# Cross attention: 32x32 squares for the results, and one turn of the maxima for two groups

## The reference, cut to what matters

```python
    def _L0_xattn_ref(values, keys, query, mask, Wv, Wk, Wq, Wo, bo):
        v = (values @ Wv.T).reshape(N, Lv, HEADS, HEAD_DIM)   # Lv = 375, 16 heads of 16
        k = (keys @ Wk.T).reshape(N, Lk, HEADS, HEAD_DIM)
        q = (query @ Wq.T).reshape(N, Lq, HEADS, HEAD_DIM)
        energy = jnp.einsum('nqhd,nkhd->nhqk', q, k)
        energy = jnp.where(mask == 0, jnp.float32(-1e+20), energy)
        attention = jax.nn.softmax(energy / jnp.sqrt(jnp.float32(E)), axis=3)
        out = jnp.einsum('nhql,nlhd->nqhd', attention, v).reshape(N, Lq, E)
        return out @ Wo.T + bo
```

## Time and profile before

| what | value |
|---|---|
| median of 3 runs | 1869.5 us (1869.06 to 1873.52) |
| profiled execution, its own time | 1868.54 us |
| its span, first to last instruction | 1867.2 us |
| mean granted clock of TensorE | 0.984 |
| PE busy | 1796.4 us (96%) |
| DVE busy | 1188.1 us (64%) |
| ACT busy | 692.4 us (37%) |
| POOL busy | 655.4 us (35%) |

### The profile page before, as it was taken

How to read it: one execution, slowest core, us unless ns; L and a number is a source line. 1 busy time by engine, 2 the same in 40 slices (tenths; PEclk the granted TensorE clock), 3 DMA queues, 4 the chain that set the end, 5 groups by cost and what they waited for, 6 DMA issues and landing times.

```text
span 1867.2 us, 39141 instructions
## 1 busy us (share of the span) xinstructions
PE 1796.4 (96%) x14764; PEld 1301.2 (70%) x14764; DVE 1188.1 (64%) x3209; ACT 692.4 (37%) x1812; POOL 655.4 (35%) x694
## 2 busy tenths in 40 slices
PE   6789999999989999999999999999999999999999
PEld 5457777776766666665445666666659979799698
DVE  4778888887657777777766676777764234243332
ACT  2234444443435555553001456565532122122221
POOL 2524444243226676664000366666624000000000
PEclk7989999999989999999999999999999999999999
DMA  6222212221031111110000010010040000000000
GB/s 202 48 42 42 45 30 42 41 37 26 13 118 52 34 45 37 33 44 12 1 1 1 11 33 23 22 32 22 12 181 1 8 3 1 11 1 1 11 1 10
DMA packets 106953, 61.94 MB, mean 33 GB/s; under 512 B 79944, under 2 KB 102800, under 8 KB 106000
## 3 DMA queue, kind: packets, MB, share of 16 engines
q1 hardware_dynamic: 106624, 59.39, 12.0%
q10 hardware_dynamic: 144, 0.06, 0.0%
HBM read 53.91 MB, written 5.51 MB: 32 GB/s over the span
## 4 chain that ended last, share of the span: by engine, by line
PE 79%; DVE 6%; issue 5%; POOL 5%; ACT 2%; DMA 2%; SPq 1%; DVEq 0%; ACTq 0%; POOLq 0%
PE ps L2515 18%; PE ps L1529 6%; PE ps L588 6%; PE ps L1551 5%; PE ps L2387 5%; PE ps L2047 5%; PE ps L1600 4%; PE ps L1568 4%; PE ps L2593 3%; PE ps L704 2%; POOL w L560 2%; PE ps L1585 2%; PE ps L1666 2%; PE ps L1538 2%; PE ps L1611 1%
## 5 line engine op out<-in xcount | busy, mean ns | idle before, releaser
L1960 POOL TENSOR_TENSOR h_w<-h_w 125x336 int32<-125x336 int32 x384 | 335.3, 902 | 205.1 <-ACT h_w L1759 205.1
L1845 DVE CUSTOM_DVE_ANT_0 h_w<-ps,h_w 112x375 f32<-112x375 f32 x512 | 262.7, 542 | 0.3 <-issue 0.3
L922 DVE SCALAR_TENSOR_TENSOR big_b<-ps,taps,big_b 128x444 f32<-128x444 f32 (+2 forms) x288 | 193.9, 674 | 55.6 <-ACT big_b L804 43.8
L1759 ACT ACTIVATE h_w<-ps 125x336 f32<-125x336 f32 x512 | 196.5, 464 | 21.9 <-PE ps L1551 21.7
L276 POOL TENSOR_TENSOR rstd<-var_eps,minus_half 112x4 f32<-112x4 f32 x12 | 12.2, 1016 | 406.5 <-DVE var_eps L263 406.5
L1551 PEld LDWEIGHTS ps<-h_w 32*125 32x125 f32 x3072 | 97.8, 184 | 68.6 <-issue 67.8
L1551 PE MATMUL ps<-h_w 32*125 32x112 f32 x3072 | 118.7, 283 | 12.4 <-DVE h_w L1845 8.3
L1529 PE MATMUL ps<-h_w 32*112 32x375 f32 x1024 | 121.0, 522 | 0.9 <-DVE h_w L1845 0.7
L588 PE MATMUL ps<-h_w,kq_w 128*128 128x448 f32 x256 | 112.3, 564 | 5.5 <-DVE h_w L942 5.5
L2047 PE MATMUL ps<-expert_w,big_a 128*112 128x512 f32 x256 | 113.6, 595 | 0.0
L1854 DVE TENSOR_TENSOR h_w<-h_w,ps 128x112 f32<-128x112 f32 x128 | 34.8, 272 | 121.6 <-PE ps L1538 121.6
(11 more groups left out here) (362 smaller groups left out, 3682.6 us busy)
## 6 DMA issues: line engine op xcount, KB each, us to landing
h_w<-in_h SPq DMA_DIRECT2D x2, 4096.0 KB, 17.6
kq_w<-in_ctxT SPq DMA_DIRECT2D x16, 375.0 KB, 3.7
h_w<-in_ctxT SPq DMA_DIRECT2D x16, 375.0 KB, 3.8
big_a<-decays SPq DMA_DIRECT2D x16, 196.0 KB, 3.1
w<-decays SPq DMA_DIRECT2D x16, 196.0 KB, 3.1
h_w<-in_mask SPq DMA_DIRECT2D x16, 164.1 KB
h_w<-in_maskT SPq DMA_DIRECT2D x16, 164.1 KB
kq_w<-in_kq_w SPq DMA_DIRECT2D x8, 256.0 KB, 3.1
```

Of the source, the lines that this page charges most:

```text
L922: dve.scalar_tensor_tensor(p3(dst)[:, :, i:], p3(ps[:, bank, 0:GT])[:, :, 0:T - i], k.taps[:, h, n, TAPS - 1 - i:TAPS - i], p3(dst)[:, :, ...
L1759: act.activation(k.PTx[(4 * Q + r) % RING][0:CK], ps[0:CK, turned_bank(Q, r), 0:NC * T], ACT.Exp).then_inc(s["exp"], 1)
L1845: dve.tensor_tensor_reduce(k.masked[r % 2], ps[0:T, score_bank(Q, r), 0:S2], k.mask_add[n % 2], -1.0, 3.0e38, ALU.add, ALU.min, k.neg_max[ ...
L1960: pool.tensor_tensor(P.bitcast(I32), P.bitcast(I32), k.mask_W[n % 2], ALU.mult).then_inc(s["weights"], 1)
```

## The change

- **32x32 squares.** DVE's transpose turns each 32x32 square. `apply` now writes each group to 128 columns of bank 6 (112 used; DVE sets the rest to 1.0 once, in the first step). `tokens` (DVE, step 3, for the sequence before) transposes bank 6, 128x512, to `o_tok` with tokens in the 32-row squares. `normalize` works on that on 128 partitions. `channels` (DVE, step 0, for the sequence two back) transposes 128x256 back to `onT` in layer 0; in layer 1 to `on_raw`, and ACT adds the bias to make `onT`, in `middle` of step 0. `output_turn`, `output_back` and ACT's copy of bank 6 are gone. The output weight keeps its own row order.
- **One turn for two groups.** `maxima` runs in steps 0 and 2 only and turns the columns of two groups, which stand in 16-column halves of the same tile. `less_maximum` becomes a `scalar_tensor_tensor` with a column of `k_keep` that keeps one half's rows, twice in a row.
- **One step later.** In step s, `maxima` and `turned` are of group s - 2, `apply` of s - 3. ACT, DVE and POOL shift alike, and each loop's tail with its first gates or experts does too. The first score of a group is ahead of the turn on PE, and the first maximum ahead of `less_maximum` on DVE. The banks of the turned scores move by two, and the waits with them.
- **Queries and values.** The last piece of the values is no longer part of `queries`: `values_2` stands at the end of step 2 and waits for the query copy. ACT copies it at the start of step 3.
- `mask_weights` moves from step 2 to step 3 on DVE.

```diff
+    turned = k.big_b[:, 0:2, :].rearrange("p a b -> p (a b)")
+    k.o_tok, k.on = turned[:, 0:XH * SQUARE], turned[:, XH * SQUARE:XH * SQUARE + XH * XD]
+    k.onT, k.on_raw = k.big_b[:, 2, 0:KD * 4 * SQUARE], k.big_b[:, 3, 0:KD * 4 * SQUARE]
@@ -1303,7 +1304,12 @@
...
-    return (8 * Q + 12 + r) % POOL_BANKS
+    return r if Q == QUADS * B - 1 else (8 * Q + 2 + r) % POOL_BANKS
@@ -1502,7 +1508,7 @@
...
-    def scores(seq, q):
...
-        for r in range(4):
+        for r in heads:
             if Q == 0 and r == 1:
                 pe.wait_ge(s["k_sb"], 4)
             if r < 2 and Q:
                 pe.wait_ge(s["max"], 4 * Q - 1 + r)
-            elif r >= 2 and Q >= 2:
-                pe.wait_ge(s["exp"], 4 * Q - 9 + r)
+            elif r >= 2 and Q >= 3:
+                pe.wait_ge(s["exp"], 4 * Q - 13 + r)
...
-        pe.wait_ge(s["max"], 4 * Q + 4)
+        pe.wait_ge(s["max"], 4 * Q + 8)
         if Q:
             pe.wait_ge(s["exp"], 4 * Q - 1)
-        pe.transpose(ps[:, turned_bank(Q, 0), NC * T:(NC + 1) * T], k.neg_max[:, q % 2, :], k.ident[0:T, 0:T]).then_inc(s["max_T"], 1)
+        pe.transpose(ps[:, turned_bank(Q, 0), NC * T:(NC + 1) * T], k.neg_max[:, Q // 2 % 2, :], k.ident[0:T, 0:T]).then_inc(s["max_T"], 1)
...
-        pe.wait_ge(s["qx"], Q + 1)
+        pe.wait_ge(s["qx"], Q + 1 if Q % 2 else Q + 2)
         if Q:
             pe.wait_ge(s["exp"], 4 * Q)
-        if Q < last:
-            pe.wait_ge(s["max"], 4 * Q + 6)
+        if Q < last - 1:
+            pe.wait_ge(s["max"], 4 * Q + 10)
@@ -1561,11 +1567,13 @@
...
             pe.wait_ge(s["V"], 2 * (n + 1))
             if n:
-                pe.wait_ge(s["oa"], n)
+                pe.wait_ge(s["o_tok"], n)
+            else:
+                pe.wait_ge(s["setup_dve"], 6)
...
-                ins = pe.matmul(ps[32 * r:32 * r + 32, 6, q * T:(q + 1) * T], k.Vx[n % 2][0:rows, c, 4 * q + r, :],
+                ins = pe.matmul(ps[32 * r:32 * r + 32, 6, q * 128:q * 128 + T], k.Vx[n % 2][0:rows, c, 4 * q + r, :],
@@ -1605,12 +1609,18 @@
...
-        pe.wait_ge(s["ctx_sum"], n + 1)
         for m in range(KD):
             for c in range(KD):
-                pe.matmul(ps[:, 7, m * T:(m + 1) * T], w["q"][:, c, m * 128:(m + 1) * 128], k.xT[:, c, 0:T],
-                          start=(c == 0), stop=(c == KD - 1))
-        values(n, 2, KD * T).then_inc(s["q_proj"], 1)
+                ins = pe.matmul(ps[:, 7, m * T:(m + 1) * T], w["q"][:, c, m * 128:(m + 1) * 128], k.xT[:, c, 0:T],
+                                start=(c == 0), stop=(c == KD - 1))
+        ins.then_inc(s["q_proj"], 1)
+
+    def values_2(seq):
+
+        n = base + seq
+        pe.wait_ge(s["ctx_sum"], n + 1)
+        pe.wait_ge(s["qz"], n + 1)
+        values(n, 2, KD * T).then_inc(s["v2_proj"], 1)
@@ -1630,40 +1640,17 @@
...
-    def output_turn(seq):
-        n = base + seq
-        pe.wait_ge(s["oa"], n + 1)
-        if is_sequence(seq + 2):
-            pe.wait_ge(s["qz"], n + 3)
-            pe.wait_ge(s["V"], 2 * n + 5)
-        elif is_sequence(seq + 1):
-            pe.wait_ge(s["V"], 2 * n + 4)
-            if l == 0:
-                pe.wait_ge(s["lnT_act"], LN_MOE + 1)
...
-        for i in range(QUADS):
-            ins = pe.transpose(ps[0:T, 7, i * 128:(i + 1) * 128], k.oa[:, i * T:(i + 1) * T], k.ident[:, :])
-        ins.then_inc(s["c_oT"], 1)
-
-    def output_back(seq):
-        n = base + seq
-        pe.wait_ge(s["on"], n + 1)
-        if seq == B - 2:
-            pe.wait_ge(s["lnT_dve"], (LN_MOE + 1, LN_FFN + KD)[l])
-        for c in range(KD):
-            ins = pe.transpose(ps[:, 7, c * T:(c + 1) * T], k.on[:, c * 128:(c + 1) * 128], k.ident[0:T, 0:T])
-        ins.then_inc(s["onT_ps"], 1)
-
     def output(seq):
         n = base + seq
         pe.wait_ge(s["onT"], n + 1)
         if is_sequence(seq + 2):
             pe.wait_ge(s["k_sb"], 4 * n + 12)
+        elif is_sequence(seq + 1):
+            pe.wait_ge(s["lnT_dve"], (LN_MOE + 1, LN_FFN + KD)[l])
+        else:
+            pe.wait_ge(s["c_x"], n)
         for c in range(KD):
-            ins = pe.matmul(ps[0:T, 7, 0:D], k.onT[:, c * T:(c + 1) * T], w["o"][:, c, :],
+            ins = pe.matmul(ps[0:T, 7, 0:D], k.onT[:, c * 128:c * 128 + T], w["o"][:, c, :],
@@ -1695,28 +1685,26 @@
...
-        elif q == 2 and is_sequence(seq - 1):
-            output_turn(seq - 1)
-        elif q == 3 and is_sequence(seq - 1):
-            if is_sequence(seq + 1):
-                pe.wait_ge(s["k_sb"], 4 * n + 6)
-            output_back(seq - 1)
+        elif q == 2 and is_sequence(seq + 1):
+            values_2(seq + 1)
 
     for step in range((B + 1) * QUADS + 1):
         seq, q = quad_at(step)
-        before, b_q = quad_at(step - 1)
-        ago, a_q = quad_at(step - 2)
+        before, b_q = quad_at(step - 2)
+        ago, a_q = quad_at(step - 3)
         if step == 1:
             values_first()
         if is_sequence(seq):
-            scores(seq, q)
-        if is_sequence(before):
+            scores(seq, q, (0,))
+        if is_sequence(before) and b_q % 2 == 0:
             maxima(before, b_q)
+        if is_sequence(seq):
+            scores(seq, q, (1, 2, 3))
         if step:
             early(seq, q)
         if is_sequence(before):
             turned(before, b_q)
-        if (seq, q) == (B, 1):
+        if (seq, q) == (B, 2):
             pe.wait_ge(s["exp"], (l + 1) * B * XH)
...
-        if (seq, q) == (B, 2):
+        if (seq, q) == (B, 3):
             if l == 0:
                 gating_pe(pe, k, s, 0, 12)
                 expert_pe(pe, k, s, 0, 2)
+                expert_pe(pe, k, s, 0, 3)
             else:
                 ffn_pe_gate(pe, k, s, 0, 2)
-        elif (seq, q) == (B, 3):
-            if l == 0:
-                expert_pe(pe, k, s, 0, 3)
-            else:
                 ffn_pe_gate(pe, k, s, 0, 3)
@@ -1762,6 +1747,11 @@
+    def values_2(seq):
+
+        n = base + seq
+        act.wait_ge(s["v2_proj"], n + 1 - (l + 1))
         if n >= 2:
             act.wait_ge(s["PV"], 4 * (n - 1))
         act.activation(k.Vx[n % 2][0:CK + 1, 2, :, 0:XD], heads_of(ps[0:CK + 1, 7, KD * T:KD * T + D]), ACT.Copy).then_inc(s["V"], 1)
@@ -1777,36 +1767,22 @@
-        elif q == 3:
-            if is_sequence(seq - 1):
-                act.wait_ge(s["onT_ps"], n)
-                if n >= 2:
-                    act.wait_ge(s["o_proj"], n - 1)
-                if l == 0:
-                    ins = act.activation(k.onT, ps[:, 7, 0:KD * T], ACT.Copy)
-                else:
-                    for c in range(KD):
-                        ins = act.activation(k.onT[:, c * T:(c + 1) * T], ps[:, 7, c * T:(c + 1) * T], ACT.Identity,
-                                             bias=k.xb_col[:, 2, c:c + 1])
-                ins.then_inc(s["onT"], 1)
+        elif l and q == 0 and is_sequence(seq - 2):
+            act.wait_ge(s["on_raw"], seq - 1)
+            act.wait_ge(s["o_proj"], n - 2)
+            for c in range(KD):
+                ins = act.activation(k.onT[:, c * 128:c * 128 + T], k.on_raw[:, c * 128:c * 128 + T], ACT.Identity, bias=k.xb_col[:, 2, c:c + 1])
+            ins.then_inc(s["onT"], 1)
...
-        before, b_q = quad_at(step - 1)
+        before, b_q = quad_at(step - 2)
...
-            if is_sequence(seq - 1):
-                act.wait_ge(s["PV"], 4 * n)
-                if n >= 2:
-                    act.wait_ge(s["c_oT"], n - 1)
-                act.activation(k.oa, ps[:, 6, 0:GT], ACT.Copy).then_inc(s["oa"], 1)
...
+            values_2(seq + 1)
             cross_keys_act(act, k, s, l, seq + 1, 0, 7)
@@ -1836,22 +1816,23 @@
         Q = 4 * n + q
         if q == 0 and r == 0:
             dve.wait_ge(s["mask"], n + 1)
-        if r == 0 and Q >= 2:
-            dve.wait_ge(s["max_T"], Q - 1)
+        if r == 0 and q % 2 == 0 and Q >= 4:
+            dve.wait_ge(s["max_T"], Q // 2 - 1)
         if 4 * Q + r >= 2:
             dve.wait_ge(s["max"], 4 * Q + r - 1)
         dve.wait_ge(s["S"], 4 * Q + r + 1)
         at = 32 * r + (XD if q % 2 == 0 else 0)
         dve.tensor_tensor_reduce(k.masked[r % 2], ps[0:T, score_bank(Q, r), 0:S2], k.mask_add[n % 2], -1.0, 3.0e38, ALU.add, ALU.min,
-                                 k.neg_max[:, q % 2, at:at + 1]).then_inc(s["max"], 1)
+                                 k.neg_max[:, Q // 2 % 2, at:at + 1]).then_inc(s["max"], 1)
 
     def less_maximum(seq, q):
         n, m, z = base + seq, q // 2, q % 2
         Q = 4 * n + q
-        dve.wait_ge(s["max_T"], Q + 1)
+        dve.wait_ge(s["max_T"], Q // 2 + 1)
         if Q >= 2:
             dve.wait_ge(s["ST"], 4 * (Q - 1))
-        dve.tensor_tensor(k.Qx[Q % 2], k.Qz[n % 2][:, z, m, :], ps[:, turned_bank(Q, 0), NC * T:(NC + 1) * T], ALU.add).then_inc(s["qx"], 1)
+        dve.scalar_tensor_tensor(k.Qx[Q % 2], ps[:, turned_bank(Q - z, 0), NC * T:(NC + 1) * T], k.k_keep[:, 2 + z:3 + z],
+                                 k.Qz[n % 2][:, z, m, :], ALU.mult, ALU.add).then_inc(s["qx"], 1)
 
```

(59 more changed lines are left out.)

50 lines of the change are left out of this document (23 added, 27 removed).

## The result

The kernel after takes 1923.4 us (median of 4 runs, 1918.89 to 1926.43), the one before on the same chip 1870.55 us: a ratio of 1.0279, 95% interval [1.0252, 1.0305]. It is 2.8% slower, where 0.9% faster was forecast. The profiled execution took 1918.89 us, its span is 1917.6, 50.4 us more than before's.

The account below looks back on a forecast made before the run. PE (busy 96%) was taken to bound the kernel. Layer 0 13.6, layer 1 1.0, first periods 3.4, fills 3.3, drains -5.6: 15.7 us off 1868.5 gives 1852.8, as median 1853.5 us; range 1843 to 1862, chance 0.60.

Parts of the forecast that it names:

- the walk along PE's queue: Layer 0's steps added piece by piece from the turn in step 0, with `keys` of step 3 ending at 15.83 us.
- The wait of the turn for ACT: Before the turn in step 0, PE waits for ACT's third exp: 0.65 us, period 18.25 instead of 17.61.
- K: End of `keys` in step 3, put at 15.83 us after the turn of step 0; next turn at K + 2.42.
- Layer 1's wait: In step 0 of layer 1, `output` on PE waits for ACT's `onT`: 1.35 us in each sequence.
- The two transposes: DVE's 128x512 and 128x256 transposes, taken as 0.61 and 0.35 us pitch; nothing up to +0.2 us on the period.
- rival C: DVE becomes the bound: transposes at 2 us give 1880 us (chance 0.05); mild form, contention with POOL, 1862 (0.05).
- A: Clock falls in layer 1's 1.35 us gaps: about 1885 us with all hit (chance 0.08), 1858 to 1875 with some (0.10).
- B: The two ACT waits don't bite: 17.6 us period in both layers, 1817 us; chance 0.12 with its half form, 1835.
- D: The turn for two groups saves nothing, its 0.5 us handed to the same wait as `output_back`; already in the sum.
- fill: Start of each layer's loop, up to its first turns: -2.4 us in layer 0 and -0.9 in layer 1.
- first periods: First sequence of each layer, without output yet: 18.78 to 17.25 and 19.18 to 17.3 us, together -3.4.
- drains: Loop ends, one step more: 35.70 to 37.9 us and 38.24 to 41.6, together +5.6, ends +1 and +9.

Follow-up runs that it names:

- squares_warm: squares_late with part of `apply` repeated as throwaway work once per layer, at the end of the loop: 1865.38 us, 0.9974 of before.
- rejoined: After with four scores ahead of the turn, bias on DVE, `tokens`/`normalize`/`channels` starting step 3, `mask_weights` in step 2, `values_2` behind queries: 1903.78 us.
- joined: The changed kernel with all four scores of a group together ahead of the turn of the maxima: 1903.83 us, 1.0183 of before.
- squares_late: Before with the 32x32 squares alone, DVE's `normalize` and `channels` ending its step 3, layer 1's bias in mid step 0: 1871.01 us, 1.0006.

## Why the prediction was wrong

**The step that failed first** is in the walk along PE's queue: "score 0.21" and "three scores 0.62", a quarter and three quarters of the block of 0.83. The row of the block gives eight matmuls in 0.83 us, the page of before 522 ns for one of them, and 8 x 522 is 4.2 us: they run side by side, and a part of the block costs as much as the block. Both numbers were there. A step of the sequence as I walked it, against the chain of after:

| step | forecast | measured | of it the scores | of it full-width products |
|---|---|---|---|---|
| 0, from the turn | 4.78 | 5.18 | +0.20 | +0.16 |
| 1 | 4.47 | 4.65 | | +0.18 |
| 2 | 4.41 | 5.57 | +0.80 | +0.37 |
| 3, with the lone score and the hold behind it | 3.90 | 4.71 | +0.60 | +0.16 |
| sum | 17.56 | 20.11 | +1.60 | +0.87 |

(The 0.08 left are the turn, 0.29 for 0.25, and 0.05 of issue; 0.01 is rounding.) The 1.60 is the split. The 0.87 is the **second error**: I priced a turn that goes at its whole 0.25 us, and leaving a place free at nothing. A product directly behind scores takes 0.17 more. So the turns removed in steps 1 and 3 gave 0.08 each. In steps 0 and 2 the split puts three scores between the turn and `keys` or `queries`: 0.35 more. And `values_2` now follows `apply`: 0.18.

**The wait of the turn for ACT** (0.65 us) is hardly there, but ACT is as late as I had it. In after, `keys` of step 3 ends at 708.41 and the turn starts at 710.83, the K + 2.42 of the forecast. Timelines of ACT (second and third exp) and of the queue of loads (that of the turn):

```profile
709.89 0.80 ACT L1744 ACTIVATE h_w<-ps 125x336 f32<-125x336 f32 x2
710.80 0.14 PEld L1544 LDWEIGHTS ps<-ident,h_w 112*128 112x128 f32 x1 [0.63 <-DVE h_w L1825]
```

The third exp ends at 710.69. DVE's last maximum ends at 710.67, K + 2.26 where I had it by K + 2.17 at the latest, and the trace puts the idle time of the load down to it; the two tie. PE's lone score ends at 710.78, at K + 2.37 instead of K + 1.77, and fills nearly all of the wait; 0.05 of issue is left. So the last leg of the sum came out, and the 0.60 too little for the score of step 3 cost nothing against the forecast. What failed lies ahead of K: it came 17.71 us after the turn of step 0 instead of 15.83, 1.88 later, which is the 1.9 by which the period was missed. PE's queue, put at 17.61 in all, was itself 20.1.

**Layer 1's wait was right**: 1.35 us forecast, 1.32 measured, in each sequence, and ended by ACT's `onT`; with it removed the run got 17 us faster. The forecast gain of almost nothing for layer 1 was wrong only by PE's own pieces: 21.63 against 19.7, 1.93 more, as in layer 0 (20.21 against 18.3, 1.91 more). (By the earlier trace rows PE idles 7.9 us in layer 1 of before and 2.8 in layer 0; I had called the 7.9 the difference, which is 5.1. No term of the sum uses it.)

**DVE was right** in its sizes. The two transposes in the timeline of after:

```profile
708.02 0.71 DVE L1851 STREAM_TRANSPOSE big_b<-ps 128x512 f32<-128x512 f32 x1
...
712.55 0.44 DVE L1868 STREAM_TRANSPOSE big_b<-big_b 128x256 f32<-128x256 f32 x1
```

They start 0.64 and 0.36 us ahead of what follows them, for 0.61 and 0.35 taken. The rule of the Trainium skill that the prediction cited (Vector Engine (DVE) Microarchitecture Reference, 3.8 The reshape front-end and per-opcode configuration) gave an estimated 0.53 plus a fixed part for 512 columns, and the trace agrees with it: 0.71, and 0.27 less for 256 columns fewer. Hidden they are in after, because PE is so long there. Where PE's blocks are mended, DVE comes next (0.67 us in step 2, the late last maximum in step 3). That was rival C with another price: not a slow transpose, but the place of `normalize`.

**The rivals.** A did not happen: 1.32 us of idle every sequence, and the granted clock is 1.00 over 281 us. Of B's first half the one branch came true: PE reaches the turn later than I had it, so the turn hardly waits, and nothing is gained by that. D, that removed work is handed to a wait, is true of another piece than I named: my sum took 0.92 us for `output_turn` and `output_back` at their full length, apart from one step's shortfall. In after they do come off (the table leaves nothing for them), but with nothing else changed they are worth 0.26, because ACT's exps need that time before the fourth head may write.

**Fills and drains.** The fill of layer 0 was -3.4 for -2.4, that of layer 1 -0.65 for -0.9. The first periods were +0.8 and +0.5 for -1.5 and -1.9, largely by the same two errors. The drains were +10.4 and +7.5 for +2.2 and +3.4. Part of that is the clock, which I had looked for in the wrong place. In after, at the end of layer 0 (timeline of PE, then a window of 6 us):

```profile
872.36 0.32 PE L1544 MATMUL ps<-ident,h_w 112*128 112x112 f32 x1 [1.44 <-DVE h_w L1825]
872.99 3.13 PE L2031 MATMUL ps<-gate_w,big_a 128*112 128x8 f32 x16 [0.31 <-DVE big_a L298]
...
873.00:879.00 6.00, 6.00 (x65) 5.45 (x65) 2.77 (x13) 1.32 (x4) 1.25 (x2) 0.50 0.00 0
```

The gating takes 3.13 us where it took 1.71 before, `turned` 1.61 for 0.92. In layer 1 the granted clock is 0.50 too, from 1409 to 1418 us. In before it is 1.00 over the 10 us from the last turn, in both layers. The last turn waits for a whole second group of maxima, with nothing left beside it. The run squares_warm shows this cause for a kernel without that turn; for after itself it was not tried, and how its 17.9 us split between clock, the step more and the later last result stays open.

**In sum**, against the forecast: 26 periods 1.92 us longer (+49.8), first periods +4.7, drains +12.3, fills -0.8; together +66.0 on the 1852.8 forecast for the profiled execution, which took 1918.9.

## What to carry to other kernels

In these traces a block of matmuls that run side by side in row quadrants has one price for one or for four of them. Don't price a part of such a block by its share, and compare the mean of one with the length of the block before splitting it. Work taken off the busiest engine is worth what is left when its neighbours' waits have grown into the hole; a repeated piece of harmless work put at the place, in the kernel before and in the one after, measures that in one run each. When work moves a step later on one engine, look at what waits for it on the others: a copy left behind holds all that stands behind it, as in rejoined. At the end of a loop look for the gaps that removed work leaves, and for the clock behind them.

## What was not expected of the hardware

- One head of scores (32 rows, 375 columns) took 0.81 us, two or three 0.82, four 0.83.
- A full-width product directly behind matmuls in quadrants took 0.16 to 0.19 us more than behind a full-width transpose (`keys` 1.46 against 1.28, both in the joined run). A 112x112 transpose put between takes 0.25, so it costs 0.08 net.
- In after, the granted clock stayed at 1.00 with an idle time of 1.32 us in each 21.6 us. In squares_late it fell (0.53 as the mean of the 6 us from 863, so nearly all of it at 1.2 GHz) after two of 0.55 and 0.49 us with only a turn between them; with the first filled and 0.33 us left of the second, in squares_warm, it stayed at 1.00. An idle time of 1.01 us some 2 us earlier is in both.
